# Another written-out order of the side work in the first attention stage of a six-stage decoder kernel

## The reference

```python
xn = (x - mu) * rsqrt(var + LN_EPS) * gamma + beta          # x: 4 batches x 512 tokens x 256
q = (xn @ Wq + bq), k = (xn @ Wk + bk)                      # 8 heads of 32
v = (xn @ Wv + bv)                                          # 8 heads of 256
p = softmax(q @ k.T / sqrt(32))
out = (p @ v).reshape(S, B, D, H).sum(axis=-1).reshape(B, S, D)
x = layernorm(x + out)
```

## Time and profile before

| | |
|---|---|
| median of 3 runs | 2714.42 us (2709.62 to 2722.24) |
| profiled execution, its own time | 2722.24 us |
| its span, first to last instruction | 2720.4 us |
| mean granted TensorE clock in it | 0.950 |
| the stage of the change in it | from 0 to 244.5 us |

### The profile page before, as it was taken

How to read it: one execution, slowest core, us unless ns; L and a number is a source line. 1 busy time by engine, 2 the same in 40 slices (tenths; PEclk the granted TensorE clock), 3 DMA queues, 4 the chain that set the end, 5 groups by cost and what they waited for, 6 DMA issues and landing times.

```text
span 2720.4 us, 40207 instructions
## 1 busy us (share of the span) xinstructions
PE 2532.3 (93%) x15290; PEld 1650.5 (61%) x15294; DVE 1414.2 (52%) x3401; ACT 1142.0 (42%) x1848; POOL 1075.0 (40%) x727
## 2 busy tenths in 40 slices
PE   6986999999999999997899999677999999989997
PEld 3433565566556555664799999655333343478886
DVE  3454555555555555554522222266788687454555
ACT  4554444444444444443222222133477677721111
POOL 5765566666665676665100000152223223010001
PEclk8998999999999999998799999889699799899998
DMA  2001000000000000000888888410010000000000
GB/s 108 10 13 56 12 18 28 13 20 13 28 18 20 13 13 13 20 7 20 307 316 319 320 309 320 137 41 18 9 30 20 18 21 13 12 20 24 24 19 33
DMA packets 61362, 188.60 MB, mean 69 GB/s; under 512 B 22617, under 2 KB 36593, under 8 KB 50289
## 3 DMA queue, kind: packets, MB, share of 16 engines
q1 hardware_dynamic: 55280, 168.70, 18.0%
q0 software_dynamic: 3584, 9.84, 1.1%
q10 hardware_dynamic: 2304, 7.49, 0.7%
HBM read 173.80 MB, written 9.70 MB: 67 GB/s over the span
## 4 chain that ended last, share of the span: by engine, by line
PE 82%; DVE 7%; issue 4%; POOL 3%; ACT 3%; DMA 0%; POOLq 0%; ACTq 0%; DVEq 0%; SPq 0%
PE PS L1502 10%; PE PS L688 8%; PE PS L2087 7%; PE PS L671 6%; PE PS L719 5%; PE PS L1513 5%; PE PS L1118 5%; PE PS L1133 4%; PE PS L729 4%; PE PS L2075 4%; PE PS L703 3%; PE PS L1151 3%; PE PS L752 2%; PE PS L675 2%; PE PS L1163 2%
## 5 line engine op out<-in xcount | busy, mean ns | idle before, releaser
L952 POOL TENSOR_TENSOR x_A<-x_A,x_P 128x1024 f32<-128x1024 f32 x190 | 451.2, 2375 | 202.9 <-ACT x_P L799 188.8
L879 DVE CUSTOM_DVE_ANT_0 x_junk<-PS,x_mb 128x512 bf16<-128x512 f32 x512 | 331.0, 685 | 352.6 <-PE PS L703 352.4
L1255 DVE TENSOR_REDUCE y_Mx<-PS 128x1 f32<-128x512 f32 x512 | 324.1, 684 | 103.5 <-PE PS L1151 101.5
L799 ACT ACTIVATE x_P<-PS,x_kb 128x1024 f32<-128x1024 f32 x256 | 271.5, 1111 | 222.8 <-PE PS L675 220.7
L1205 ACT ACTIVATE y_P<-PS 128x1024 f32<-128x1024 f32 x256 | 257.3, 1025 | 99.9 <-PE PS L1133 97.4
L1502 PEld LDWEIGHTS PS<-m_xt,m_w 128*128 128x128 f32 x2496 | 287.3, 193 | 2.9 <-issue 0.9
L1502 PE MATMUL PS<-m_xt,m_w 128*128 128x128 f32 x2496 | 287.7, 276 | 0.6 <-issue 0.6
L688 PE MATMUL PS<-x_P,x_V 128*64 128x512 f32 x1024 | 249.1, 608 | 0.0
L671 PE MATMUL PS<-x_Q,x_K 64*128 64x512 f32 x1536 | 228.3, 400 | 0.0
L2087 PE MATMUL PS<-n_xp,n_wp 128*128 128x512 f32 x816 | 211.8, 409 | 4.3 <-POOL n_wp L2203 4.3
L1692 DVE SCALAR_TENSOR_TENSOR m_h<-PS,m_bc,m_g 128x128 f32<-128x128 f32 x312 | 87.9, 344 | 212.9 <-PE PS L1502 212.8
(11 more groups left out here) (324 smaller groups left out, 4117.8 us busy)
## 6 DMA issues: line engine op xcount, KB each, us to landing
m_w<-in_m_w SPq DMA_DIRECT2D x39, 2048.0 KB, 8.1
m_v<-in_m_w SPq DMA_DIRECT2D x39, 1024.0 KB, 5.3
x_w<-in_x_w SPq DMA_DIRECT2D x32, 384.0 KB, 3.0
ys<-m_yb SPq DMA_DIRECT2D x39, 128.0 KB, 5.3
n_wg<-in_n_w SPq DMA_DIRECT2D x17, 256.0 KB, 2.9
x_cT<-in_ctxT SPq DMA_DIRECT2D x4, 1024.0 KB, 6.6
y_c<-in_ctxT SPq DMA_DIRECT2D x6, 512.0 KB, 3.6
n_wd<-in_n_w SPq DMA_DIRECT2D x17, 128.0 KB, 2.0
```

Of the source, the lines that this page charges most:

```text
L799: act.e.activation(Pt[gt % 6][:], PS[:, 2 * i:2 * i + 2, :], ACT.Exp, bias=kb[u // 8 % 2][:, kt:kt + 1], scale=scale).then_inc(s["exp"], 1)
L879: dve.e.tensor_tensor_reduce(junk[j % 2][:], ring.bank("max", v, j), mb[b % 2][:, half * 512:half * 512 + 512], 1.0, -3e38, ALU.add, ALU.m ...
L952: pool.e.tensor_tensor(A[u % 2][:], Pt[(gt - 1) % 6][:] if kt == 1 else A[u % 2][:], Pt[gt % 6][:], ALU.add).then_inc(s["add"], 1)
L1255: dve.e.tensor_reduce(Mx[v % 2][:, h, qt, half:half + 1], ring.bank("max", v, j), AX.X, ALU.max).then_inc(s["red"], 1)
```

## The change

Only the written-out order changes. No instruction is added or removed.

```diff
--- before.py
+++ after.py
@@ -233,18 +233,18 @@
 
 
             at = {
-                0: [("pv", 0, 0), ("max", 1, 2), ("ev", -1, 0), ("ot", -3, 3), ("max", 1, 3), ("mul", -2, 0), ("k", 2, 0)],
-                1: [("pv", 0, 1), ("max", 1, 4), ("den", -1, 0), ("max", 1, 5), ("q", 2, 0), ("st", -3, 0)],
-                2: [("pv", 0, 2), ("max", 1, 6), ("ot", -2, 0), ("max", 1, 7), ("v", 2, 0), ("rec", -1, 0), ("nr", -3, 0)],
-                3: [("pv", 0, 3), ("max", 2, 0), ("turn", 1, 0), ("tp", -3, 0), ("ot", -2, 1), ("max", 2, 1), ("ot", -2, 2), ("tp", -3, 1)],
+                0: [("k", 2, 0), ("max", 1, 2), ("pv", 0, 0), ("ev", -1, 0), ("max", 1, 3), ("st", -3, 0)],
+                1: [("q", 2, 0), ("max", 1, 4), ("den", -1, 0), ("pv", 0, 1), ("mul", -2, 0), ("max", 1, 5), ("nr", -3, 0)],
+                2: [("tp", -3, 0), ("v", 2, 0), ("max", 1, 6), ("pv", 0, 2), ("max", 1, 7), ("ot", -2, 0), ("ot", -2, 1)],
+                3: [("tp", -3, 1), ("turn", 1, 0), ("max", 2, 0), ("pv", 0, 3), ("max", 2, 1), ("rec", -1, 0), ("ot", -2, 2),
+                    ("ot", -2, 3)],
             }
-            once = {(0, 0): [("v", 0, 0)], (0, 1): [("v", 1, 0)], (0, 3): [("prefetch", 0, 0)],
+            once = {(0, 0): [("v", 0, 0), ("tp0", 1, 0), ("tp0", 1, 1)], (0, 1): [("v", 1, 0)], (0, 3): [("prefetch", 0, 0)],
                     (1, 1): [("st0", 2, 0)], (1, 2): [("nr0", 2, 0)], (1, 3): [("tp0", 2, 0), ("tp0", 2, 1)],
-                    (3, 1): [("st0", 3, 0)], (3, 2): [("nr0", 3, 0)], (3, 3): [("tp0", 3, 0), ("tp0", 3, 1)]}
-            first = ([("st0", 0, 0), ("nr0", 0, 0), ("tp0", 0, 0), ("tp0", 0, 1), ("st0", 1, 0), ("k", 0, 0), ("q", 0, 0), ("sums", 0, 0),
-                      ("nr0", 1, 0), ("max", 0, 0), ("max", 0, 1), ("k", 1, 0), ("max", 0, 2), ("max", 0, 3), ("q", 1, 0),
-                      ("max", 0, 4), ("max", 0, 5), ("tp0", 1, 0), ("tp0", 1, 1), ("max", 0, 6), ("max", 0, 7), ("max", 1, 0),
-                      ("turn", 0, 0), ("max", 1, 1)])
+                    (2, 2): [("st0", 3, 0)], (2, 3): [("nr0", 3, 0)], (3, 0): [("tp0", 3, 0), ("tp0", 3, 1)]}
+            first = ([("st0", 0, 0), ("nr0", 0, 0), ("tp0", 0, 0), ("tp0", 0, 1), ("k", 0, 0), ("q", 0, 0), ("sums", 0, 0)]
+                     + [("max", 0, j) for j in range(4)] + [("k", 1, 0)] + [("max", 0, j) for j in range(4, 8)]
+                     + [("turn", 0, 0), ("q", 1, 0), ("max", 1, 0), ("max", 1, 1), ("st0", 1, 0), ("nr0", 1, 0)])
 
             def windows():
                 return [(-1, 0)] + [(u, t) for u in range(n) for t in range(T)] + [(n, t) for t in range(T)]
@@ -252,7 +252,7 @@
             def side(u, t):
                 if u < 0:
                     return first
-                o = []
+                o = list(once.get((u, t), ()))
                 for name, du, i in at[t]:
                     v = u + du
                     second = name in ("ot", "st", "nr", "tp") and v % 2 == 0
@@ -261,8 +261,6 @@
                         o.append((name, u, t))
                     elif name != "pv" and 0 <= v < n and not (second or later):
                         o.append((name, v, i))
-                    if name == "max" and i % 2 == 1:
-                        o += once.get((u, t), ())
                 return o
 
             for u, t in windows():
```

## The result

The changed kernel takes 2743.94 us (median of 4, 2740.5 to 2750.24) where the kernel before takes 2716.76 (now a median of 4, with one run more than in the table ahead of the prediction); the ratio is 1.0109 (95% interval 1.0072 to 1.0147). It is slower by about 27 to 30 us, where 13 were forecast with a range up to +28. The direction was the likelier one; the size was off by a factor of two, and the time lies 2 us above the range of 2715 to 2742.

A forecast was written before the change was run, and what follows sets the result against it. No engine is full: a loop over PE, ACT and DVE through four banks bounds the stage. Steady windows +4.3, start +10.4, end -4.7 sum to +10.0; 3 for clock falls gives +13, 2727.5 us, range 2715 to 2742.

The forecast's parts named there:

- The steady windows: Units 1 to 5: windows 6.3, 7.3, 6.35 or 6.9, and 5.6 us; together 129.7 against 125.4, so +4.3.
- the price list: Times of PE items at full clock, start to start: scores 1.14, den 0.99, max 0.43, k or q 1.91, v 1.98 us.
- I add 3 for one or two falls to half clock more than the old order had: Clock term for the windows ending in a bare wait of 1.3 us, raising the sum from +10.0 to +13 us.
- the four cases: The rivals: clock falls in most bare waits (0.15), cheaper start (0.12), faster (0.08), and change does nothing.
- the first rival: Clock falls in most of about 18 bare waits; two thirds falling gives +27, 2741 us; chance 0.15.
- The start: Head of the stage: late q and norm delay scores (0, 1) to 54.6; unit 1 starts at 74.8 for 64.44, +10.4.
- The end: From unit 6 on: POOL starts its sums sooner and waits for data; 49.9 us instead of 54.6, so -4.7.
- The moved ot items: Windows 2 and 3: ot fits the second wait, its DVE additions end before the next first max; that cost is gone.
- The reading that the head position of k, q, v spends this gain: Units 1 to 5: nearly all that the freed DVE gives is spent on the bare second wait; +4.3.
- The faster rival: Second wait not bare, some 18 windows each lose up to 1.3 us; -10, 2704 us; chance 0.08.
- the rival of a cheap start: Start: the norm's chain lies beside other work as DVE is free earlier; +5, 2719 us; chance 0.12.
- the three signs of being wrong: Scores (0, 1) before 50, middle units under 24 us, or granted clock of units 1 to 5 below 0.85.

The follow-up runs named there:

- e5: The changed kernel plus one matmul of no use in every bare wait of units 0 to 5; ratio to the kernel before 1.0101, median 2736.2 us.
- e13: e1 plus the one-matmul filler of e5 in the bare waits of units 0 to 5; ratio to the kernel before 1.0030, median 2730.6 us.
- e1: The changed kernel with the old start: list `first` of before, transposes of batch 1 back in it; ratio to the kernel before 1.0079, median 2740.9 us.
- e14: The same kernel as e1, run for a second profile; ratio to the kernel before 1.0084, median 2742.1 us.
- e6: Kernel before with ot, st, mul and rec at their new places, both tp behind window 3's max items; ratio 0.9984, median 2705.0 us.
- e12: The kernel before with only ot moved, behind the second max of windows 2 and 3; ratio to the kernel before 0.9994.
- e2: The kernel before, its table kept, with the new list `first` (q of unit 1 and norm of batch 1 both late); ratio 1.0057.
- e7: The kernel before with only q of unit 1 moved behind turn in `first`; ratio to the kernel before 1.0026.
- e8: The kernel before with only the norm of batch 1 at the end of `first`, its transposes in window (0, 0); ratio 1.0059.
- e9: e6 plus e5's filler in window 3 of units 0, 2, 4 and windows 0 to 2 of unit 6; ratio 0.9954, median 2709.3 us.
- e10: e9 plus four extra matmuls of 128x256 behind max items in `first`; ratio to the kernel before 0.9978.
- e11: The kernel before plus the filler of e9, and so also in windows 1 and 2; ratio to the kernel before 0.9993.
- e4: The changed kernel with k, q, v behind the second max again and pv at the head of each window; ratio to the kernel before 1.0039.

## Why the prediction was wrong, point by point

**The steady windows were right, the clock was not.** At full clock the price list gave 129.7 us for units 1 to 5, and e5 and e13 measured 129.45 and 129.46. The term that failed is "I add 3 for one or two falls to half clock more than the old order had". The profile after has seven windows with a fall in these units, five windows 1 and windows (1, 0) and (3, 0), each 1.5 to 1.7 us longer than in e5: 140.7 - 129.45 = 11.3 us where 3 were allowed, so 8 of the 16 missing us are here. The sum has a slip in the same term: its 129.7 is at full clock, while the 125.4 of the old order holds about 3 us of falls, so adding 3 gave the new order as many falls as the old one and not one or two more. And the fall that was priced at 1.9 "between 42.79 and 45.9" shows k with 3.10 us for 1.98, 1.1 more; the measured 1.5 to 1.7 still lies inside the two prices.

The nearest of the four cases was the first rival, the clock falling in bare waits. It had 2741 us and a chance of 0.15, and it was put too low. Its own count, two thirds of the waits, was too high: in units 1 to 5 there are 17 scores rows with 1.32 us or more of idle time before them, and 7, 2 and 6 windows with a fall in the profiles of after, e1 and e14. That its total came so near is in part luck, since the start added 6 us that it hadn't.

I had argued against it with one row, the wait of 204.49 with 1.32 idle that came in at full clock, and with units 4 and 5, at 1.00 "with waits in every window". The trace of before said otherwise. From unit 1 to unit 6 it has six scores rows with more than 1.3 us of idle time before them, at 64.44, 113.30, 189.86, 196.59, 204.49 and 209.78. Those at 113.30, 196.59 and 209.78 come in at half clock or fall to it at once, the clock falls 1.3 us behind that at 64.44 (window (1, 0) has 0.58), and the row that I chose lies in a stretch at full clock of 6.8 us between two at half. The longest such wait in units 4 and 5 is 0.93 us:

```profile
113.30 1.52 PE L309 MATMUL PS<-a_Q,a_K 32*128 32x512 f32 x12 [1.59 <-DVE a_Mq L446]
...
146.18 0.97 PE L309 MATMUL PS<-a_Q,a_K 32*128 32x512 f32 x12 [0.93 <-DVE a_Mq L446]
...
196.59 1.65 PE L309 MATMUL PS<-a_Q,a_K 32*128 32x512 f32 x12 [2.83 <-DVE a_Mq L446]
...
209.78 1.66 PE L309 MATMUL PS<-a_Q,a_K 32*128 32x512 f32 x12 [1.54 <-DVE a_Mq L446]
```

A filler took away falls in these places too. Of the six profiles with the table of before or of e6 or e12 and no filler ahead (before, e2, e6, e7, e8, e12), five fell in (1, 0), all but e2, and five in (3, 0), all but e12, with 6.44 to 6.66 us there; the three with a filler (e9, e10, e11) fell in neither, with 5.63 to 5.65 us.

**The start: the right mechanism, 6 us too small.** Foreseen was unit 1 at 74.8 against 81.14. The rows of the profile after:

```profile
24.08 3.32 PE L357 MATMUL PS<-xT,a_wk 128*128 128x512 f32 x4
...
32.93 1.09 PE L350 MATMUL PS<-ident,a_Mq 128*128 128x128 f32 x4 [1.85 <-DVE a_Mq L444]
33.81 3.62 PE L357 MATMUL PS<-xT,a_wq 128*128 128x512 f32 x4
...
41.31 1.40 DVE L112 BATCH_NORM_STATS2 st<-x 128x6 f32<-128x256 f32 x4
...
41.55 1.65 PE L307 MATMUL PS<-a_Q,a_K 32*128 32x512 f32 x12 [2.54 <-DVE a_Mq L444]
...
45.07 2.08 ACT L145 ACTIVATE a_xh<-x,shift,rstd 128x256 f32<-128x256 f32 x4 [6.33 <-POOL shift L136]
...
47.05 1.91 ACT L397 ACTIVATE a_P<-PS 128x1024 f32<-128x1024 f32 x2
...
50.92 2.80 PE L357 MATMUL PS<-xT,a_wk 128*128 128x512 f32 x4 [3.00 <-ACT xT L182]
...
56.90 1.65 PE L307 MATMUL PS<-a_Q,a_K 32*128 32x512 f32 x12 [2.45 <-DVE a_Mq L444]
```

q takes 3.62 us (forecast 3.8), scores (0, 0) come at 41.55 (40.0), the normalization at 45.07 (43.7), the exponentials at 47.05, and scores (0, 1) at 56.90 (54.6). Up to there 2.3 us are missing. The first 1.6 were there before q began: the sum took turn from the old order, at 31.35, and it came at 32.93, since k of unit 1, now ahead of the max items 4 to 7, took 3.32 us at half clock, where the q that stood ahead of the same reductions before took 1.98. Another 0.8 is k of unit 2 with 2.80 for 1.98, the case that the prediction named and didn't take. The other 4 us lie in windows (0, 1) and (0, 2), 10.48 and 7.94 us for 8.3 and 6.35, at a clock of 0.75 and 0.79: clock again. With the old start and filler the windows of unit 0 behind the first take 8.08, 6.37 and 5.81 (e13).

**The end: right in kind, 1.9 us too large.** POOL came to its rstd for batch 1 7.4 us after the start of unit 6 (229.24), where it was 16.4 (it still waited 5.67 us for the statistics there), and its first sum of unit 7 waited for ACT, not for its own backlog, as forecast:

```profile
229.24 0.23 POOL L127 TENSOR_SCALAR rstd<-mv 128x4 f32<-128x4 f32 x1 [5.67 <-DVE mv L115]
...
253.13 4.72 POOL L481 TENSOR_TENSOR a_A<-a_P 128x1024 f32<-128x1024 f32 x2 [1.37 <-ACT a_P L397]
...
267.19 0.23 POOL L127 TENSOR_SCALAR rstd<-mv 128x4 f32<-128x4 f32 x1
...
273.06 0.66 ACT L180 ACTIVATE xT<-PS 128x256 f32<-128x256 f32 x2 [0.32 <-PE PS L170]
```

From rstd at 267.19 to the end are 6.5 us (forecast 5.9, as before from 238.60), and unit 6 took 25.58 us instead of 23.4, once more for a window 1 of 8.75 at a clock of 0.61. The round through memory and the scaling cost nothing: POOL scaled at 250.47 and then waited for ACT until 253.13.

**The moved ot items** did what was said: windows 2 and 3 of odd units take 6.36 and 5.81, for 6.56 and 6.84, and e12 shows 2.9 us for them alone in units 3 to 5. **The reading that the head position of k, q, v spends this gain** holds by e4: a unit at full clock is some 2 us shorter once they stand behind the max again, and with the falls the end of the stage comes 27 us earlier. **The faster rival** and **the rival of a cheap start** are dead: every scores row behind a bare wait in the profile after names DVE, and (0, 1) started later than even the forecast had it. **None of the three signs of being wrong** showed: (0, 1) started behind 50, middle units took over 24 us, and the clock of units 1 to 5 was 0.92 together, 0.88 at the lowest. A bound of 0.85 was too low to catch a term that allowed 3 us of falls in 130.

By the ends of the stages the parts add up roughly: the start alone +10.3 (e2), the rest alone +14.8 and +17.8 (e1, e14), both +29.2. What stays open is how often a given execution falls in this stage. The profiles show one execution each. The timed runs have a granted clock on record too, 0.941 to 0.951 for the changed kernel, with the faster runs mostly at the higher values, but as a mean over the whole launch, of which this stage is a tenth.

## What to carry to other kernels

In a loop over several engines, ask of each wait what covers it before moving work between them: here the exponentials' wait had pv to cover it already, and the reductions' wait, the last before the next scores, was left with nothing. Before moving an item to the end of a list, look at every engine that walks the list; an item that ends on an in-order engine holds up all that this engine does next. And where PE gets a bubble in every round, price it twice, once as time and once as clock, with all rows of the profile that have such a bubble as the measure and not with a single quiet one; a filler in the bubble is a cheap test of which of the two it is.

## What the runs showed of the hardware

- With a wait of 1.32 us in most windows of 6 to 7 us, PE fell to 1.2 GHz about once in a unit of 27 us in the profile after (clock 0.94 in units 2, 4 and 5), and twice in five units in e1. One added matmul (1.12 us in the trace) in each wait, without use and without moving the next scores, left it at 2.4 GHz for all of units 1 to 5, in both profiles that had it (e5, e13); of the fifteen units without it (after, e1, e14) three were at full clock. It is no guarantee: in e11 window (4, 3) and in e10 window (6, 1) fell with a filler in or just ahead of them. The Trainium skill (TensorE: Matmul & The Clock Gate, A second HAM failure mode: psum-queue depth-cycling) tells of a kernel with short idle times between its groups of matmuls, in which the clock swings; the trace agrees, and shows it for waits of 1.32 us.
- The same program fell in some places in one execution and not in another: units 2, 4 and 5 took 25.63, 26.01 and 25.64 us in e1, and 27.23, 27.61 and 28.76 in e14.
